# CIN tower with top network: two 32-row steps ahead of 64-row steps, the top network spread over the steps

## The reference, cut to what matters

```python
x0 = embeddings                                    # (1024, 32, 16)
xk = x0
for W in (W0, W1, W2):                             # 64 maps each
    xk = relu(einsum('bmd,bhd,mhk->bkd', x0, xk, W))
    outs.append(sum(xk, axis=2))
z = concatenate(outs, axis=1)                      # (1024, 192)
h = concatenate([z, dense_ctx], axis=1)            # 208 columns
h = relu(h @ W_top1 + b_top1)                      # 512
h = relu(h @ W_top2 + b_top2)                      # 256
y = h @ W_top3                                     # 1
```

## Time and profile before

| | us |
|---|---|
| median of 3 runs | 637.69 (637.17 to 637.77) |
| the profiled execution | 638.89 |
| its span in the trace | 637.1 |
| VectorE / TensorE / GpSimd / ScalarE busy | 548.7 / 563.1 / 488.3 / 302.5 |

### The profile page before, as it was taken

The page is one execution under the profiler, slowest core; times in us unless marked ns, Lnnn a source line. Parts: engine busy times, 40 slices in busy tenths (PEclk is TensorE's granted clock), DMA queues, the critical chain, the costliest instruction groups (busy, mean ns, idle before and its releaser), DMA issues.

```text
span 637.1 us, 7625 instructions
## 1 busy us (share of the span) xinstructions
PE 563.1 (88%) x2440; PEld 178.9 (28%) x2440; DVE 548.7 (86%) x330; ACT 302.5 (47%) x1359; POOL 488.3 (77%) x364
## 2 busy tenths in 40 slices
PE   0058998999999998999899999999999989999998
PEld 0012232332323232332223232323232322333332
DVE  0038998999999999999999999999999999897810
ACT  0023637354545646364535456464736454544352
POOL 6756898869888888979898788888897989584500
PEclk9997999999999999999999999999999999999999
DMA  3298857677876867686778768686868587871000
GB/s 105 39 391 312 307 200 284 240 298 263 306 274 227 295 217 270 244 299 214 297 274 306 268 238 315 211 298 215 307 213 319 225 302 266 307 284 49 1 1 0
DMA packets 52843, 151.01 MB, mean 237 GB/s; under 512 B 9697, under 2 KB 17377, under 8 KB 52802
## 3 DMA queue, kind: packets, MB, share of 16 engines
q1 hardware_dynamic: 44610, 148.40, 63.6%
q0 software_dynamic: 8192, 2.11, 2.5%
HBM read 147.33 MB, written 3.15 MB: 236 GB/s over the span
## 4 chain that ended last, share of the span: by engine, by line
DVE 36%; PE 24%; DMA 19%; issue 10%; POOL 8%; SPq 2%; ACT 1%; DVEq 0%; POOLq 0%
DVE prod L286 34%; PE y_ps L417 20%; DMA x0bc<-x_rows 15%; POOL emb L247 6%; DVE z L314 2%; DMA emb<-table,row_sb 2%; DMA x_rows<-emb 2%; POOL pool_prod L260 1%; SPq L214 1%; PE x_ps L477 1%; ACT relu L373 1%; PE x0g_ps L477 1%; PE x_ps L470 1%; PE x0g_ps L470 1%; PE x0g_ps L471 1%
## 5 line engine op out<-in xcount | busy, mean ns | idle before, releaser
L286 DVE TENSOR_TENSOR prod<-x0bc,x_ps 128x2048 f32<-128x2048 f32 (+1 forms) x252 | 456.0, 1878 | 8.6 <-ACT x_ps L368 8.6
L417 PE MATMUL y_ps<-prod,w_sb 128*64 128x512 f32 x1640 | 384.9, 599 | 27.8 <-DVE prod L286 27.8
L247 POOL DMA_INDIRECT emb<-table,row_sb x256 | 244.9, 957 | 65.5 <-issue 63.7
L260 POOL TENSOR_TENSOR pool_prod<-x0bc,x_sb 128x1024 f32<-128x1024 f32 x102 | 242.3, 2382 | 45.7 <-ACT x_sb L383 36.3
L417 PEld LDWEIGHTS y_ps<-prod,w_sb 128*64 128x64 f32 x1640 | 115.5, 137 | 280.1 <-issue 219.7
L373 ACT ACTIVATE relu<-y_ps 128x16 f32<-128x16 f32 x512 | 84.5, 287 | 144.3 <-PE y_ps L417 144.3
L368 ACT ACTIVATE x_ps<-y_ps 64x512 f32<-64x512 f32 x128 | 73.0, 570 | 78.5 <-PE y_ps L417 75.8
L417 PE MATMUL y_ps<-pool_prod,w_sb 128*64 128x512 f32 x408 | 105.0, 595 | 1.5 <-POOL pool_prod L260 1.3
L286 DVE TENSOR_TENSOR prod<-x0bc,x0g_ps 128x2048 f32<-128x2048 f32 x32 | 72.6, 2282 | 38.5 <-DMA x0bc<-x_rows 35.3
L373 ACT ACTIVATION_READ_ACCUMULATOR relu<-y_ps 128x1 f32 x512 | 84.7, 315 | 0.2
L383 ACT ACTIVATE x_sb<-relu 64x512 f32<-64x512 f32 x128 | 80.4, 628 | 3.4
(11 more groups left out here) (29 smaller groups left out, 49.2 us busy)
## 6 DMA issues: line engine op xcount, KB each, us to landing
x0bc<-x_rows SPq DMA_DIRECT2D x256, 512.0 KB, 6.8
x0g<-x_rows SPq DMA_DIRECT2D x16, 512.0 KB, 4.7
emb<-table,row_sb POOLq DMA_INDIRECT x256
x_rows<-emb SPq DMA_DIRECT2D x16, 128.0 KB, 2.1
w_sb<-w SPq DMA_DIRECT2D x2, 512.0 KB, 4.6
x_rows<-emb SPq DMA_DIRECT2D x16, 64.0 KB, 2.0
x0bc<-wt SPq DMA_DIRECT2D x1, 512.0 KB, 5.4
x0bc<-wt_a SPq DMA_DIRECT2D x1, 256.0 KB, 4.1
```

The lines of the kernel that those rows point to most:

```text
L247: pool.indirect_dma_start(emb[:, turn, DIM * n:DIM * (n + 1)], None, table, bass.IndirectOffsetOnAxis(row_sb[:, at:at + 1], 0)).then_inc(g ...
L260: pool.tensor_tensor(pool_prod[:, n % POOL_RING, :], x0bc[:, slot(s, j), :], x[:], ALU.mult).then_inc(pool_products, 1)
L286: made = dve.tensor_tensor(prod[:, n % RING, 0:count, cols], tiles[:, :, cols], right.unsqueeze(1).to_broadcast([P, count, right.shape[1]] ...
L417: made = pe.matmul(ps[MAPS * h:MAPS * (h + 1), :], w, moving[:, HALF * h:HALF * (h + 1)], start=first, stop=final)
```

## The change

Steps are 32, 32, then 15 times 64 rows (17 steps), all widths following the step. GpSimd forms no products in step 0 and, before its loop, issues the gathers of steps 0, 1 and 2 (8 + 8 + 16, as many as before). The top network has buffers of its own; its loads are issued after step 1's tiles. It runs in five chunks of steps (256, 256, 256, 192, 64 rows): a chunk's inputs are copied by ScalarE at the start of the step behind it, TensorE does the first layer before that step's layer 2, the second behind it, and the output in the next step's layer 1, behind the first group; the fourth chunk lies wholly inside the last step. The chunks use x0g_ps as PSUM. Each chunk's y is stored from ScalarE's queue. In the last step ScalarE does one relu over all of layer 2 and VectorE sums it; the last chunk has 64 rows.

```diff
+ROWS_OF = [32, 32] + [64] * 15
+POOL_OF = {0: (0, 0), STEPS - 2: (5, 4), STEPS - 1: (5, 4)}
+CHUNKS = [(0, 5), (5, 9), (9, 13), (13, 16), (16, 17)]
+TURN = {end: c for c, (_, end) in enumerate(CHUNKS[:FINAL])}
...
 sync, in the loop over s
                 load_tiles(s)
-            sp.wait_ge(products, after((LAST - 1, 2)))
-            sp.wait_ge(pool_products, pool_after((LAST - 1, 2)))
-            for dst, src in (... the 7 loads of the top network ...):
+                if s == 1:
+                    for dst, src in (... the same 7 ...):
+                        sp.dma_start(dst, src).then_inc(mlp_in, 16)
...
 gpsimd
-            gather(0, 0, GATHERS)
+            gather(0, 0, GATHERS_OF[0])
             pool.wait_ge(rows_done, 2)
-            gather(1, 0, GATHERS)
+            gather(1, 0, GATHERS_OF[1])
+            gather(2, 0, GATHERS_OF[2])
...
 vector
-            mlp_input(1)
+            sums(LAST, 2)      # one TENSOR_REDUCE, waits for the relu
+            last_input()       # two copies of 64 x 32 into zt_b
...
 scalar, in the loop over s
+                if s - 1 in TURN:
+                    hidden2(TURN[s - 1])           # 2 activations
+                    output(TURN[s - 1])            # 1, and the store
+                if s in TURN:
+                    mlp_input(TURN[s], range(3))   # 6 copies (12 for chunk 0)
                 if s < LAST:
                     place_x0g(s + 1)
                     square(s + 1)
                 finish(s, 1, x2_ps, x2_sb)
                 if s < LAST:
                     finish(s + 1, 0, x1_ps, x1_sb)
-                else:
-                    mlp(range(MLP_EARLY))
+                if s in TURN:
+                    hidden1(TURN[s])               # 4 activations
+                if s == LAST:
+                    hidden2(TURN[s])
+                    output(TURN[s])
+                    mlp_input(FINAL, range(2))
                 finish(s, 2)
-            mlp(range(MLP_EARLY, len(MLP)))
+            hidden1(FINAL)
+            hidden2(FINAL)
+            output(FINAL)
...
 tensor
+            def hidden1(c):
+                pe.wait_ge(zt_ready, inputs_after(c))
+                for j in range(H1_TILES):          # 4: 8 matmuls of n columns
+                    pe.matmul(ps, wt1a_sb[:, out_f], zt_a[:, 0:n], start=True, stop=False)
+                    made = pe.matmul(ps, wt1b_sb[:, out_f], zt_b[:, b], start=False, stop=True)
+            def hidden2(c):
+                pe.wait_ge(mlp_act, PIECES_OF_CHUNK * c + H1_TILES)
+                ...                                # 2 x 4 matmuls of n columns
+            def output(c):
+                pe.wait_ge(mlp_act, PIECES_OF_CHUNK * c + H1_TILES + H2_TILES)
+                ...                                # 2 matmuls of n columns
+            def last_chunk():                      # 64 columns: zt_a's 4 matmuls,
+                ...                                # wait zt_last, zt_b's 4, then 8, then 2
             for s in range(STEPS):
-                layer(s, 1, w1_sb)
+                layer(s, 1, w1_sb, {1: lambda: output(TURN[s - 1])} if s - 1 in TURN else {})
                 if s < LAST:
                     layer0(s + 1)
+                if s in TURN:
+                    pe.wait_ge(mlp_in, 16 * 7)
+                    hidden1(TURN[s])
+                if s == LAST:
+                    layer(s, 2, w2_sb, {2: lambda: hidden2(TURN[s]), 4: lambda: output(TURN[s])})
                 else:
-                    pe.wait_ge(mlp_in, 16 * 7)
-                    mlp(range(MLP_EARLY))
-                layer(s, 2, w2_sb)
-            mlp(range(MLP_EARLY, len(MLP)))
+                    layer(s, 2, w2_sb)
+                    if s in TURN:
+                        hidden2(TURN[s])
+            last_chunk()
```

More of the change, by code:

```diff
@@ L44, with columns, width, half @@
 POOL_RING = 4
-POOL_LAST = {STEPS - 2: (5, 4), STEPS - 1: (5, 4)}
-POOL_COUNT = [POOL_LAST.get(s, (3, 3)) for s in range(STEPS)]
-POOL_BEFORE = {3: [2, 3, 5], 4: [2, 3, 4, 5], 5: [2, 3, 4, 5, 5]}
+POOL_OF = {0: (0, 0), STEPS - 2: (5, 4), STEPS - 1: (5, 4)}
+POOL_COUNT = [POOL_OF.get(s, (3, 3)) for s in range(STEPS)]
+POOL_BEFORE = {0: [], 3: [2, 3, 5], 4: [2, 3, 4, 5], 5: [2, 3, 4, 5, 5]}
 GATHERS_AFTER = {1: [1, 1, 8], 2: [1, 1, 4]}
+def columns(s):
+    return slice(DIM * FIRST_ROW[s], DIM * FIRST_ROW[s + 1])
+def width(s):
+    return DIM * ROWS_OF[s]
+def half(s):
+    return width(s) // 2
 def pool_tiles(s, l):
@@ L279, in _, with product @@
         def _(dve):
-            def product(n, count, tiles, x, h=None):
+            def product(s, n, group, x, h=None):
                 if n >= RING and h != 1:
                     dve.wait_ge(products_used, n - RING + 1)
[L284 to L287, removed]
+                at, count = slot(s, group[0]), len(group)
+                halves = slice(0, 2) if h is None else slice(h, h + 1)
+                out, left = (t.rearrange("p t (h c) -> p t h c", h=2)[:, :, halves, :]
+                             for t in (prod[:, n % RING, 0:count, 0:width(s)], x0bc[:, at:at + count, 0:width(s)]))
+                right = x[:, halves, 0:half(s)].unsqueeze(1).to_broadcast(list(left.shape))
+                made = dve.tensor_tensor(out, left, right, ALU.mult)
                 if h != 0:
@@ new lines, in mlp_input @@
+            def mlp_input(c, layers):
+                first = FIRST_ROW[CHUNKS[c][0]]
+                for l in layers:
+                    if l == 2:
+                        act.wait_ge(relu_done[2], summed2_after(CHUNKS[c][1] - 1))
+                    else:
+                        act.wait_ge(summed[l], CHUNKS[c][1])
+                    for a, end in runs(c):
+                        rows = slice(FIRST_ROW[a], FIRST_ROW[end])
+                        dst = zt_b[0:MAPS, rows] if l == 2 else (
+                            zt_a[MAPS * l:MAPS * (l + 1), rows.start - first:rows.stop - first])
+                        dst = dst.rearrange("p (s h b) -> p s h b", s=end - a, h=2)
+                        for h in range(2):
+                            src = z[MAPS * h:MAPS * (h + 1), l, rows.start // 2:rows.stop // 2]
+                            act.activation(dst[:, :, h, :], src.rearrange("p (s b) -> p s b", s=end - a),
+                                           ACT.Copy).then_inc(zt_ready, 1)
@@ new lines, in hidden2, with output @@
+            def hidden2(c):
+                n = CHUNK_ROWS[c]
+                pe.wait_ge(mlp_act, PIECES_OF_CHUNK * c + H1_TILES)
+                for j in range(H2_TILES):
+                    for k in range(H1_TILES):
+                        made = pe.matmul(x0g_ps[:, 0, CHUNK_B * j:][:, 0:n], wt2_sb[:, k, P * j:P * (j + 1)],
+                                         h1[:, k, 0:n], start=k == 0, stop=k == H1_TILES - 1)
+                made.then_inc(mlp_mm, 1)
+            def output(c):
+                n = CHUNK_ROWS[c]
+                pe.wait_ge(mlp_act, PIECES_OF_CHUNK * c + H1_TILES + H2_TILES)
+                for k in range(H2_TILES):
+                    made = pe.matmul(x0g_ps[0:1, 1, 0:n], wt3_sb[:, k:k + 1], h2[:, k, 0:n], start=k == 0,
+                                     stop=k == H2_TILES - 1)
+                made.then_inc(mlp_mm, 1)
@@ L512 @@
         "table": np.concatenate([get[f"tbl_{f}"] for f in range(FIELDS)], axis=0),
[L513 to L514 removed]
+        "ids": np.concatenate([get["ids"].T[:, FIRST_ROW[s]:FIRST_ROW[s + 1]].reshape(P, -1) for s in range(STEPS)],
+                              axis=1),
+        "id_offset": np.repeat(offsets, QUART)[:, None],
         "dense_t": get["dense_ctx"].T,
```

256 lines of the change are left out of this document (140 added, 116 removed).

## The result

The changed kernel takes 655.85 us (median of 4 runs, 653.65 to 657.13) against 637.73 for the kernel before on the same chip: a ratio of 1.0278, interval 1.0246 to 1.0309. The forecast was 631.9 with a range to 641, so it was wrong in sign.

What follows compares the result with a forecast made beforehand. VectorE was taken to bound the middle, TensorE having 2 us to spare. Span 637.1 - 7.0 (start) - 16.8 (end) + 18 (chunks) = 631.3, by the median 631.9; range 619 to 641, the forecast's own 625 to 637.

Steps and rivals of the forecast that it cites:

- The start: From the first loads to step 2: half-width first steps bring the work forward, a gain of 7.0 us.
- VectorE's layer 1 starts at about 29: Step 0: first product at 24.1, TensorE's half-width layer 0 takes 3 us, then VectorE begins layer 1 at about 29.
- Step 2's x0g is then loaded at 56.6: Step 2's store follows step 1's last tiles (49.6) and seven loads (3 us); its x0g is loaded at 56.6.
- half the bytes: Step 0: x0g's issue to VectorE's first product takes 5.4 us, between 3.9 and 7.8.
- Rival C: The start brings nothing: GpSimd's first step starts at 59 instead of 52, the 7.0 us go, 638.9; chance 8 in 100.
- The chunks: Three 256-row top-network chunks inside steps: output waits behind ScalarE's relus, costing 6 us each, 18 in all.
- Rival A: The chunks fit into TensorE's spare time at 2 us each, giving 619.9; chance 17 in 100.
- Rival B: Weight loads show at 256 columns, 0.4 us an instruction, 10.8 a chunk, giving 651, slower; chance 13 in 100.
- The end: Last step and top network: a 64-row tail of 10.4 us replaces 28.55, net gain 16.8 us.

Runs made afterwards that it cites:

- paced: The changed kernel with step 2's gathers in two runs of 8, behind the copies of layers 0 and 1 of step 0; ratio 1.0157.
- hold2: The changed kernel with GpSimd waiting for the spread of step 0's layer 0 before issuing step 2's 16 gathers; 656.38 us, ratio 1.0262.
- no_chunks: The changed kernel without the top network for rows 0 to 767, whose outputs are not computed; 640.04 us, ratio 0.994.
- after_again: The changed kernel once more, unaltered; 662.09 us in a single run.
- paced_mlp3: As paced, with the top network's seven loads issued behind step 3's tiles instead of step 1's; ratio 1.0186.
- holdload: The changed kernel with SyncE waiting for the spread of step 0's layer 0 before issuing step 1's tile loads; 652.96 us in one run.

## Why the prediction was wrong, point by point

*The start, the step that failed: "VectorE's layer 1 starts at about 29", and from it "Step 2's x0g is then loaded at 56.6".* Three things were mis-sized.

1. I costed the hand-over from TensorE to ScalarE at nothing while GpSimd's run of gathers goes on. In five of the six half-step profiles with an unbroken run of 32 the spread came 1.5 to 6.3 us behind that run's end; only in the profile shown above it came 3.3 ahead of it. In the earlier trace rows TensorE's layer 0 ended at 44.99 (38.80 + 6.19) and the gathers at 44.27, so the two could not be told apart. I left the 32 gathers as they were and moved layer 0 to 13 us before their end, where the wait shows in full.
   What followed from it: VectorE's layer 1 began at 41.70, 12.7 later than 29. Of these, 2.45 are TensorE's end (31.45, from the later first product of point 3), 9.4 the hand-over (to 40.86) and 0.84 lie between the spread and the product. Layer 2 of step 0 was then 11.8 late (56.26; 44.5 forecast).
2. The chain from there to step 2 was too short as well. Step 2's x0g was 16.2 late (72.75), 4.4 more than layer 2 of step 0, and these 4.4 are SyncE's: step 1's last tile went out at 62.60 (37.61 + 24.99; 49.6 forecast), the seven loads and the gap took 4.55 rather than 3, and from the store to x0g it took 5.6 rather than 4. From layer 2 of step 0 to layer 0 of step 2 it takes 24.8 us (56.26 to 81.08), 19.9 forecast, and 29.5 in paced. A half-width tile takes a whole slot, so 24 slots look ahead half as long: VectorE has two layers between, about 30 us of work with full steps, 18 with half ones. How much of this belongs to the slots, to the rows and to the seven loads was not taken apart. Avoiding the late wake of layer 0 gave nothing in hold2 (1.0262) and 1.2% at most in paced (1.0157 from 1.0278), which delays the rows as it does so.
3. For half the bytes I took 5.4 us from x0g's issue to the first product; it took 8.2 (18.34 to 26.50), above the old 7.8 for the whole. The rate accounts for little of that: 2 KB rows move at 269 GB/s with the DMA engines busy for 0.94, 4 KB rows at 390 with 1.02, so half the bytes take 0.72 of the time (390/269, halved), 5.6 us. The rest stays open. In the other profiles with half steps the same piece took 5.9 to 7.4; the 8.2 is the longest of all.

Rival C named the place, and step 2's order, but as a gain of nothing; a loss of 10.7 was in no rival. The granted clock was 0.50 (1.2 GHz) from 34.9 to 48.5, in and after TensorE's pause of 11.68 us, against 6.8 us of it before, but it is not seen to set the path. VectorE did wait 2.66 us in layer 1 (49.13), but for a place in the ring that TensorE had emptied by about 44.8 (8 of the 32 instructions from 43.13): that too is a late wake, though the run of gathers was over by 44.2.

*The chunks.* The working stands nearly to the tenth of a us. From 226.00: hidden1 makes way at 5.3 (5.2 predicted), hidden2 starts at 19.2 (19.1), ScalarE's hidden2 at 24.4 behind the relus (its end predicted at 25.5, measured 25.4), output to 26.5 (26.4), spread at 38.8, next layer 2 at 40.8 (39.9). The three long steps are 40.8, 39.7 and 39.9, 16.1 over three times the old average of 34.78; the steps behind them lose 1.2, 1.9 and 3.0, where I took 1. So 22.2 instead of 18, and 7.2 a chunk by no_chunks. The mechanism was right, the term 20% small. Rival A falls. Rival B falls as well: 16 matmuls of 256 columns with as many weight loads took 3.72, 0.23 each, not 0.4. By the Trainium skill (TensorE: Matmul & The Clock Gate, The mechanism) weight loads overlap only where the row group differs; the same section also lets them go ahead into the background weight buffer. Here all rows are the same and the loads are hidden, so the first of these sentences does not hold as it stands.

*The rest of the middle*, 27.1 - 22.2 = 4.9: the three steps from 115.47 to 226.00 took 110.5 against 104.3, the others 1.3 less than average. One of these holds a stall of VectorE of 3.6 us, in layer 2 of step 4, and it is a late spread again, behind a run of 8 gathers:

```profile
181.34 2.75 PE L501 MATMUL y_ps<-prod,w_sb 128*64 128x512 f32 x12
...
186.13 0.94 POOL L282 DMA_INDIRECT emb<-table,row_sb  x1 [0.30 <-issue]
...
189.13 2.35 ACT L406 ACTIVATE x_ps<-y_ps 64x512 f32<-64x512 f32 x4 [9.00 <-PE y_ps L501]
```

TensorE ended layer 1 at 184.09 (181.34 + 2.75), the run of gathers at 187.07, and the spread came 5.0 behind TensorE. In after_again it did not.

*The end.* Layer 1 to layer 2 of the last step took 22.0 (22.3 predicted), the relu to the span's end 8.0 rather than 10.4: the hand-overs and the store were quicker. Right, and a little better.

What stays open: why a run of gathers keeps ScalarE waiting. The trace has the time of ScalarE's wake, not whether TensorE's last matmul ends late (its ends are modelled) or only its semaphore arrives late. VectorE's waits for TensorE are hit as well, and somewhat after a run too: 49.13 in the changed kernel (its run ended at 44.2), 61.39 in paced (59.43). And in paced_mlp3 TensorE itself seems to stumble beside a run: five instructions of layer 1 stand about 0.7 us apart between 74.06 and 77.32, where they otherwise come 0.14 apart. Nor does every run of gathers do it: in the steady steps GpSimd issues 8 in a row, and from step 2 on the spread of layer 1 follows TensorE within 0.5 us in 13 of 14 steps; the stall at 189.13 is the other. And with the late wake of layer 0 avoided, in hold2 and paced, most of the start's loss is still there, so what share of the 17.7 us it has by itself stays open too.

## What to carry to other kernels

A first step cut in half is worth only what the chain behind it can use: count in buffers, not in bytes, how far the loads may run ahead, and check that every look-ahead still covers the latency it used to. Before you move work under a stream of gathers that another engine has covered until now, look at who waits while it runs. Breaking the stream into pieces makes what it carries later: in paced the rows of step 2 were what SyncE waited for, from 59.01 to 64.23. Work put into another engine's spare time costs what its last hand-over waits for; in pieces over several steps the same top network took 15.9 us less.

## What the runs showed of the hardware that was not expected

ScalarE's wake by TensorE while GpSimd issues gathers back to back came up to 20 us late (after_again 50.49, TensorE's layer 0 ended at 30.42), and 15.5 us in hold2. VectorE's wake by TensorE was late shortly after such runs too (49.13 in the changed kernel, after 2.66 idle; 61.39 in paced, after 4.49), and the DMA engines were nearly idle in holdload (0.07) while the spread waited. VectorE's products reached TensorE during the run of gathers without such a delay: in the changed kernel the first ended at about 27.7 (26.50 + 1.21) and TensorE began at 27.77. And rows of 2 KB came at 0.69 of the rate of rows of 4 KB, the DMA engines as busy.
